# One VectorE maximum over two neighbouring PSUM banks, returned by one semaphore, in an attention and gated-FFN kernel

## The reference, cut to what matters

```
xn = layernorm(x)
q, k, v = split(xn @ W_attn + b_attn)            # 16 heads of 16
q, k = rope(q), rope(k)
att = softmax(where(causal, q @ k.T / sqrt(16), -inf))
s = (att @ v) @ W_proj + b_proj
h = silu(xn @ w_gate.T / 127) * (xn @ w_up.T / 127)
out = x + s * silu(h @ w_down.T / 127)
```

## Time and profile before

| | us |
|---|---|
| median of 3 runs | 1216.95 |
| lowest and highest | 1214.07, 1217.84 |
| the profiled execution's own time | 1217.21 |
| its span, from first to last instruction | 1215.5 |
| TensorE, weight loads apart, busy | 1126.6 |
| VectorE busy | 1007.0 |
| ScalarE busy | 890.8 |
| GpSimd busy | 770.5 |

### The profile page before, as it was taken

How to read it: one execution, slowest core, us unless ns; L and a number is a source line. 1 busy time by engine, 2 the same in 40 slices (tenths; PEclk the granted TensorE clock), 3 DMA queues, 4 the chain that set the end, 5 groups by cost and what they waited for, 6 DMA issues and landing times.

```text
span 1215.5 us, 27634 instructions
## 1 busy us (share of the span) xinstructions
PE 1126.6 (93%) x9484; PEld 454.6 (37%) x9484; DVE 1007.0 (83%) x3092; ACT 890.8 (73%) x1708; POOL 770.5 (63%) x942
## 2 busy tenths in 40 slices
PE   3779999999999999999999999999999999999996
PEld 2223333434334343434334243433434343343433
DVE  6689989988989888888899878898898987989822
ACT  4458777777877778778787777777787786878774
POOL 3536546496836948289564867469492894747672
PEclk9989999999999999999999999999999999999999
DMA  6160041503342151611525024331515115240201
GB/s 175 61 162 11 11 125 63 133 25 99 71 142 62 27 142 33 172 29 35 144 72 134 11 72 108 111 95 28 142 33 171 31 32 146 71 97 15 61 2 53
DMA packets 71281, 97.51 MB, mean 80 GB/s; under 512 B 18398, under 2 KB 44388, under 8 KB 71140
## 3 DMA queue, kind: packets, MB, share of 16 engines
q1 hardware_dynamic: 71072, 95.73, 28.8%
q10 hardware_dynamic: 68, 0.01, 0.0%
HBM read 52.76 MB, written 34.47 MB: 72 GB/s over the span
## 4 chain that ended last, share of the span: by engine, by line
PE 55%; DVE 14%; POOL 14%; ACT 6%; issue 6%; DMA 3%; SPq 2%; POOLq 0%; DVEq 0%; ACTq 0%
PE ring L931 27%; PE acc L922 12%; PE st L871 8%; PE ring L898 6%; DVE ring L1293 4%; POOL xn L579 4%; POOL pexp L1597 3%; DVE mx_s L1297 3%; POOL hf L1627 2%; DMA q_st<-mT 2%; ACT pexp L1127 2%; SPq L640 2%; DVE ga L1357 1%; DVE ln L1320 1%; ACT parts L1169 1%
## 5 line engine op out<-in xcount | busy, mean ns | idle before, releaser
L1127 ACT ACTIVATE pexp<-st 128x512 f32<-128x512 f32 x1152 | 623.6, 598 | 141.3 <-PE st L871 138.6
L1293 DVE CUSTOM_DVE_ANT_0 ring<-ring,tri 128x512 f32<-128x512 f32 (+3 forms) x1024 | 470.5, 522 | 36.6 <-PE ring L898 35.6
L1597 POOL TENSOR_SCALAR_AFFINE_SELECT pexp<-pexp 128x512 f32<-128x512 f32 x256 | 158.0, 635 | 347.2 <-ACT pexp L1127 254.0
L1297 DVE TENSOR_REDUCE mx_s<-ring 128x1 f32<-128x512 f32 x512 | 326.3, 681 | 42.7 <-PE ring L898 41.1
L922 PE MATMUL acc<-pexp,v_pad 128*17 128x512 f32 (+3 forms) x3072 | 303.7, 490 | 12.5 <-POOL pexp L1597 10.2
L898 PE MATMUL ring<-k_st,q_st 56*128 56x512 f16 (+4 forms) x1536 | 239.7, 327 | 20.7 <-DVE g L1365 11.0
L871 PE MATMUL st<-q_st,k_st 58*128 58x512 f16 (+3 forms) x1536 | 235.1, 332 | 13.2 <-DMA q_st<-mT 6.6
L871 PEld LDWEIGHTS st<-q_st,k_st 58*128 58x128 f16 x1536 | 61.9, 93 | 288.3 <-ACT pexp L1127 184.5
L1293 DVE DVE_READ_ACCUMULATOR2_ANT mx_s<- 128x1 f32 x1024 | 145.2, 142 | 0.0
L1627 POOL TENSOR_TENSOR hf<-ga,ups 128x512 f32<-128x512 f32 x96 | 121.9, 1274 | 6.8 <-DVE ga L1357 5.6
L922 PEld LDWEIGHTS acc<-pexp,v_pad 128*17 128x17 f32 x3072 | 61.4, 96 | 148.7 <-issue 119.4
(11 more groups left out here) (152 smaller groups left out, 1330.0 us busy)
## 6 DMA issues: line engine op xcount, KB each, us to landing
parts_scratch<-parts SPq DMA_DIRECT2D x32, 512.0 KB, 2.9
q_st<-parts_scratch SPq DMA_DIRECT2D x62, 192.0 KB, 3.8
k_st<-parts_scratch SPq DMA_DIRECT2D x62, 192.0 KB, 4.5
parts_scratch<-parts SPq DMA_DIRECT2D x32, 256.0 KB, 3.6
xo<-in_x SPq DMA_DIRECT2D x32, 256.0 KB, 3.4
out<-xo SPq DMA_DIRECT2D x32, 256.0 KB, 2.2
xn<-in_x SPq DMA_DIRECT2D x7, 1024.0 KB, 7.3
yn<-yT SPq DMA_DIRECT2D x224, 32.0 KB
```

Of the source, the lines that this page charges most:

```text
L1127: nc.scalar.activation(pexp[:, GH * (n % NSET) + j, :], st[:, (GH * n + j) % NST, :], ACT.Exp, scale=1.0 / (QK_SCALE * np.sqrt(D))).then_i ...
L1293: top_ = nc.vector.tensor_tensor_reduce(out=src, in0=src, in1=tri[:, CH - w:CH], scale=1.0, scalar=NEG, op0=ALU.add, op1=ALU.max, accum_ou ...
L1297: top_ = nc.vector.reduce_max(dst, src, AX.X)
L1597: nc.gpsimd.affine_select(out=t, in_=t, compare_op=ALU.is_ge, fill=0.0, base=0, pattern=[[0, GH], [1, P]], channel_multiplier=-1).then_inc ...
```

## The change

For F items whose two banks are neighbours (the second bank's number is the first's plus one, so first banks 0, 1 and 2, not 3), VectorE waits for both heads' scores and takes both maxima in one `tensor_reduce` over 2 x 512 elements, with an output of 2 elements a partition. That instruction increments `ring_free` of the first bank alone. `FREES` counts what is given back by each semaphore, without the second head of such items, and `wait_done` looks up the first bank's semaphore for either head. TensorE's `take` can't subtract one from a bank's use number any more, since the use before may have been given back by another bank's semaphore; `use_before` finds that use, and `take` waits for its giving back.

```diff
+def both_heads(kind, task):
+
+    if task[0] != "MX":
+        return False
+    found = SEGMENTS[max_of(kind, 0, task[1])[2], task[2]]
+    t, k0, w, _ = found[0]
+    return w == CH and k0 + w < (t + 1) * P and BANK[kind, task, 1] == BANK[kind, task, 0] + 1
+
+
+FREES = [Tally(lambda k, t, b=b: [(t, name) for name in names_of(k, t)
+                                  if BANK[k, t, name] == b and not (name == 1 and both_heads(k, t))])
+         for b in range(NRING)]
...
         def wait_done(eng, kind, i, task, name=""):
 
-            eng.wait_ge(ring_free[bank(kind, task, name)], use(kind, i, task, name))
+            if name == 1 and both_heads(kind, task):
+                name = 0
+            b = bank(kind, task, name)
+            eng.wait_ge(ring_free[b], FREES[b].at(kind, i, (task, name)))
+
+        def use_before(kind, i, task, name):
+
+            b = bank(kind, task, name)
+            n = USES[b].seen[kind].index((task, name))
+            while n == 0:
+                before = body_before(kind, i)
+                if before is None:
+                    return None
+                kind, i = before
+                n = len(USES[b].seen[kind])
+            return (kind, i) + USES[b].seen[kind][n - 1]
...
             def take(kind, i, task, name=""):
 
                 b = bank(kind, task, name)
-                wait(pe, ring_free[b], use(kind, i, task, name) - 1)
+                before = use_before(kind, i, task, name)
+                if before:
+                    wait_done(pe, *before)
                 return ring[:, b, :], ring_ready[b]
...
+                if both_heads(kind, t_ring):
+                    t, _, _, p = found[0]
+                    b = bank(kind, t_ring, 0)
+                    for a in range(2):
+                        wait_ready(dve, kind, i, t_ring, a)
+                    nc.vector.tensor_reduce(mx_s[:, par, p:p + 3:2, t, 0:1], ring[:, b:b + 2, :], AX.X, ALU.max)\
+                        .then_inc(ring_free[b], 1)
+                    return
                 for a in range(2):
                     b = bank(kind, t_ring, a)
                     wait_ready(dve, kind, i, t_ring, a)
```

## The result

The changed kernel takes 1244.73 us (median of five runs, 1243.17 to 1251.39) against 1216.95 us. The ratio, which goes by all runs and not by the medians alone (these give 1.0228), is 1.0248, 95% interval 1.0221 to 1.0274. That is slower, as forecast, by 28 us where the forecast had 20. The median lies inside the range of 1226 to 1246 us; the ratio puts the time at 1217 x 1.0248 = 1247, one microsecond above its upper end. Taken again later beside another kernel, the changed one measured 1244.84 us, 1.0244 (1.0221 to 1.0267).

A forecast was written before the change was run, and what follows sets the result against it. The prediction took hand-offs between in-order engines, chiefly ring banks returned to TensorE, as the bound: 1217.2 us + 12.4 (returns less small gains) + 7.9 (takes in six middle batches) = 1237.5, rounded 1237, range 1226 to 1246.

The forecast's parts named there:

- The joined reduce: VectorE's reduce of 2 x 512 elements: 1.21 us against 1.28 for the pair, saving 12 us of work over 173.
- The two waits: VectorE waiting for both heads before one instruction: later start costs nothing, extra wait 7 us at most, taken as nothing.
- The late bank: First head's bank returned to in-order TensorE 0.53 us later; takes starting within 0.58 us of the release are pushed.
- The sum in the middle batches: Six middle batches: chain returns at 0.53 us each, plus takes in TensorE's stretches at 1.3 us a batch.
- the 25 returns: Chain returns to TensorE from a changed pair's first reduce, over the span: 0.53 us each, 13.3 us.
- 7.9 us of takes: Just-in-time bank takes within TensorE's long chain stretches: 1.3 us in each of six middle batches.
- the second UPU product: Take after the pair at 618.75: TensorE comes 0.53 late to a bank 0.46 late, so it adds nothing.
- I let these two cancel: First and last batch: a few more pushed takes, set against gains of 0.07 us ahead of some returns; net nothing.
- The chain alone: Rival: takes in TensorE's stretches are swallowed, only returns count, 1229.6 us; chance 0.20, shared with a shorter joined reduce.
- All takes add: Rival: 104 of 173 first banks are taken again within 0.58 us, pushes sum to 37 us, 1254 us; chance 0.10.
- VectorE is the bound: Rival: the bank has room, so VectorE's 12 us come off whole, 1205 us; chance 0.05.
- the two cancel: Rival: fewer pairs joined than counted, or banks' lateness falls into idle time as often as VectorE's gain; 1217 us, 0.07.

The follow-up runs named there:

- both waits: Kernel before, but in the 173 pairs VectorE waits for both heads' scores ahead; each reduce returns its own bank: 1216.48 us, 1.0013.
- tight pairs: Changed kernel, joining only the 110 pairs whose first bank was taken again within 0.60 us in the kernel before: 1244.33 us, 1.0246.
- roomy pairs: Changed kernel, joining only the 63 pairs whose first bank was taken again no sooner than 0.60 us in the kernel before: 1216.75 us, 1.0010.
- middle and last: Changed kernel, with pairs joined only in the six middle batches and the last one (136 pairs): 1236.28 us, 1.0182.
- prologue: Changed kernel, with pairs joined only in the prologue (9 pairs): 1216.88 us, 1.0028.
- half width: Changed kernel, joined reduce over 2 x 256 instead of 2 x 512 elements, maxima over key columns 256 to 511 left out: 1211.10 us, 0.9979.
- one return: Changed kernel, with two reduces of 512 elements instead of the joined one, both banks returned by the second's semaphore: 1251.13 us, 1.0301.
- prologue and first: Changed kernel, with pairs joined only in the prologue and the first batch (37 pairs): 1224.05 us, 1.0088.
- first alone: Changed kernel, with pairs joined only in the first batch (28 pairs): 1223.56 us, 1.0064.

## Why the prediction was right or wrong, point by point

**What bounds the kernel: right.** The end is set by returns of ring banks to an in-order TensorE, not by VectorE's work. Half the width in the joined reduce took away 94 us of VectorE's work and brought 3 us; a late return of the first bank, with all of VectorE's work kept, cost 37.

**The joined reduce: right.** Estimated 1.21 us, measured 1.219. The work saved was put at 12 us and is 9.2 in these groups, 0.053 us an instruction. The Trainium skill's fixed cost of 0.125 us for each PSUM-source instruction ("VectorE: DVE Perf Modes", TRN2 errata) would have made it an estimated 22: the trace doesn't agree. Another figure of the Trainium skill, some 75 ns an instruction after queue overlap and 1.0417 ns a column ("Vector Engine (DVE) Microarchitecture Reference", section 5.2), is near what the rows show: (1.219 - 0.681) / 512 = 1.05 ns a column, and an estimated 0.61 us from one reduce of 512 columns to the next by its figures, where the rows have 0.60.

**The two waits: right**, by the kernel with both waits and separate returns. The 0.04 us that were to bound the extra wait bound nothing: in the earlier trace rows they lie between the start of a readout and the start of the product, and the readout takes 0.15.

**The late bank: right in size.** 0.53 was the price of a return; the steps by which the shift grows are 0.53 and 0.54.

**The sum in the middle batches: near as a sum, in part by luck, since two terms trade places.** By the prediction's terms, 21 of the 25 returns and 7.9 us of takes, the six middle batches cost 18.4 us; they cost 18.3 to 20.3 in four profiles (19.4 with the tight pairs is the fourth) against the one of before, and some 21 against an average one. But the second UPU product of the earlier trace rows, which was said to add nothing, adds 0.36: it stands 6.27 us behind the first there (613.22, 619.49) and 6.63 on the chain of after (635.55, 642.18). The argument was that VectorE works without a gap up to it and so isn't late itself. It doesn't stay so. VectorE's timeline in the kernel before, where the items between the two pairs follow each other:

```profile
615.16 0.14 DVE L1293 DVE_READ_ACCUMULATOR2_ANT mx_s<- 128x1 f32 x1
615.16 0.73 DVE L1293 CUSTOM_DVE_ANT_0 ring<-ring,tri 128x512 f32<-128x512 f32 x1
...
616.45 0.15 DVE L1293 DVE_READ_ACCUMULATOR2_ANT mx_s<- 128x1 f32 x1
616.55 0.57 DVE L1293 CUSTOM_DVE_ANT_0 ring<-ring,tri 128x384 f32<-128x384 f32 x1
```

and in the changed kernel:

```profile
636.90 0.14 DVE L1332 DVE_READ_ACCUMULATOR2_ANT mx_s<- 128x1 f32 x1
637.17 0.70 DVE L1332 CUSTOM_DVE_ANT_0 ring<-ring,tri 128x512 f32<-128x512 f32 x1
...
638.43 0.14 DVE L1332 DVE_READ_ACCUMULATOR2_ANT mx_s<- 128x1 f32 x1
638.70 0.57 DVE L1332 CUSTOM_DVE_ANT_0 ring<-ring,tri 128x384 f32<-128x384 f32 x1
```

From the start of a readout to the start of the next reduce it is now 0.27 us twice, where it was none and 0.10: TensorE, pushed at the first UPU product, delivers the next scores late, VectorE waits for them, and its next return is late by that much more. Against this the V product of the later batches, a return on the chain of before (665.05 in the earlier trace rows), adds nothing in the batches looked at: the pair ahead of it had been pushed at the UPU product already.

**The step that failed: "the first and last batch have a few more such takes; against them stand small gains of 0.07 ahead of some returns. I let these two cancel."** By the prediction's terms the prologue and the first batch together cost 1.3 us, three returns less their small gains. The first batch alone costs 6.1. Its takes could be read from the trace of before, as those of the middle batches were: 17 of its 28 pairs have a first bank that is taken again within 0.58 us, and the pushes add up to 5.5 us, where the forecast kept three returns; gains of 0.07 don't cancel that. Of the 6.1 us some 4.3 to 4.8 are such takes. That is most of the difference, and it is a term mis-sized, not another mechanism. The other 1.3 to 1.8 us are TensorE's clock at the start of the batch, which the prediction didn't look at, and which the last section shows. The last batch is the same omission: five pushes of 1.2 us in sum, 1.0 to 1.3 measured, 0.5 by the forecast. What the joined pairs cost within the prologue stays open.

**The rivals.** "The chain alone" (1229.6) is out by the takes in TensorE's stretches: they are on the chain of after by name. "All takes add" (1254) is nearer than it looked. By the trace of before its 37 us fall to 5.5 in the first batch, 28 in the middle ones and 1.2 each in the prologue and the last batch; the first and last batches pay nearly all of theirs, the middle ones some 18 to 21, since lateness is given back there. "VectorE is the bound" and "the two cancel" are out by the kernels above. It did do what it says.

No version beat the kernel before by an amount that can be told: the roomy pairs alone are the same, and the one that is 0.2% faster leaves work out.

## What to carry to other kernels

A ring buffer returned in larger pieces is returned later: ask of each piece when its first part was taken again, and give the late part the price of every take that starts right behind a release. Work saved on an engine counts only where that engine's end releases something that is waited for; here 94 us of VectorE's work were worth 3 us, and 0.54 us of lateness at 110 pairs cost 30. Where a stretch has the same order of work as the one that was priced, count its takes too, and don't let takes of 0.5 us cancel against gains of 0.07.

## What the runs showed of the hardware that was not expected

By way of TensorE's clock one wait cost more here than its length. At the end of the prologue TensorE is granted half its clock, 1.2 of 2.4 GHz, and gets the full level back some microseconds into the first batch. Stretches of 2 us (length, then each engine's busy time, granted clock, DMA), first in the kernel before, then in the second profile of the changed one:

```profile
80.00:82.00 2.00, 2.00 (x12) 0.72 (x10) 2.00 (x5) 1.89 (x5) 0.56 (x1) 0.50 0.98 197
82.00:84.00 2.00, 2.00 (x10) 0.51 (x8) 1.60 (x9) 0.89 (x2) 1.05 (x2) 0.68 1.11 356
84.00:86.00 2.00, 1.99 (x25) 0.82 (x24) 1.79 (x4) 1.73 (x5) 0.68 (x2) 1.00 1.09 217
```

```profile
80.00:82.00 2.00, 1.59 (x12) 0.66 (x10) 1.90 (x3) 1.89 (x4) 0.99 (x2) 0.50 1.07 245
82.00:84.00 2.00, 2.00 (x8) 0.45 (x8) 1.35 (x8) 0.26 (x2) 0.63 (x1) 0.50 1.10 348
84.00:86.00 2.00, 2.00 (x14) 0.29 (x10) 1.58 (x4) 1.41 (x3) 0.42 (x1) 0.50 1.08 201
86.00:88.00 2.00, 2.00 (x21) 0.98 (x18) 0.86 (x3) 0.86 (x2) 0.80 (x2) 0.59 0.64 137
```

From 80 to 82 us TensorE was busy without a break in the kernel before, 2.00 of 2 us; in the changed one it stood 0.41 us, before the first UPG product, for the joined reduce. The full level comes back in the stretch from 82 us there and from 86 us here. The same value products, in the timeline of before and of the changed kernel, one at full and one at half clock:

```profile
84.02 1.05 PE L922 MATMUL acc<-pexp,v_pad 128*17 128x512 f32 x8
```

```profile
81.87 0.61 PE L962 MATMUL ring<-xh,w_ga 128*128 128x512 f16 x1 [0.41 <-DVE mx_s L1321]
...
84.65 1.91 PE L953 MATMUL acc<-pexp,v_pad 128*17 128x512 f32 x8
```

The step at the UPG product is 0.48 us; the half clock behind it adds 1.8 us more (0.32, 1.28 and 0.17 at the next three takes), in all four profiles with the first batch joined. Some 0.5 us are given back by the gate product that starts at 92.05 us of before, ahead of which TensorE itself stood 0.38 us for VectorE there. So of the first batch's 6.1 us some 1.3 to 1.8 are clock and 4.3 to 4.8 takes.

The other kernels bear out that late banks bring the longer half clock. From the first maxima product of the first batch to the return of the full level, by the granted clock of each profile, it takes (us):

```
first batch's tight banks in time   before 4.4, both waits 4.8, roomy pairs 6.1, middle and last 4.2, prologue 5.4, half width 5.6
first batch's tight banks late      changed 9.3, again 9.2, one return 9.3, tight pairs 9.2, prologue and first 8.9, first alone 9.2
```

The six profiles of either kind don't overlap, though the prologue's shift varies over nearly 8 us among them. That it is this one break ahead of the UPG product is argued: it is the only step of more than 0.2 us between the start of the batch and the return of the full level in the kernel before, and no kernel had this break alone.
